# A state-space stage on one core: the scan's decay factors move into one ring of six buffers, made four units ahead

## What is computed

```python
hs, gate = split(einsum('blh,eh->bel', x, Win))            # 512 channels each
hs   = silu(conv4(hs) + bconv)
dt_in, Bm, Cm = split(einsum('bdl,pd->blp', hs, Wx))       # 128, 16, 16
dt   = softplus(einsum('blr,dr->bld', dt_in, Wdt) + bdt)
dA   = exp(A * dt)                                         # A = -exp(A_log), per channel and state
dBu  = dt * Bm * hs
h_t  = dA_t * h_(t-1) + dBu_t                              # per channel, state and step
y_t  = sum over the 16 states of h_t * C_t
y    = (y + hs * D) * silu(gate);  out = y @ Wout.T;  x = x + out
```

## Time and profile before

| | us |
|---|---|
| median of 3 runs | 4711.3 |
| lowest and highest run | 4702.89, 4714.27 |
| the profiled execution, its own time | 4701.33 |
| its span in the trace | 4699.5 |
| mean granted clock of TensorE, share of full | 0.939 |

### The profile page before, as it was taken

One profiled execution on the slowest core, in us unless ns is written; L12 is line 12 of the kernel. 1 busy time (PEld: TensorE's weight loads), 2 busy tenths in 40 slices (PEclk: granted clock), 3 DMA queues, 4 the chain that ended last, 5 costly groups with the idle time before them and its releaser, 6 DMA issues. The chain is left out here.

```text
span 4699.5 us, 147070 instructions
## 1 busy us (share of the span) xinstructions
PE 4031.9 (86%) x63660; PEld 2779.2 (59%) x63668; DVE 3046.8 (65%) x5625; ACT 2381.8 (51%) x4795; POOL 1496.9 (32%) x1590
## 2 busy tenths in 40 slices
PE   7627886678887887899799999999999998689999
PEld 6415654345565765344477777767776776455555
DVE  7897744757776887764577777777777776521111
ACT  3446533667776555322566666666666665221111
POOL 1001200168896221000344444444434443112222
PEclk9868987889998999999899999999999999789999
DMA  1000000123342000100110000001001000041111
GB/s 35 19 27 11 2 13 21 51 86 127 125 130 97 2 2 15 40 1 0 47 26 22 25 22 25 22 21 26 22 22 28 22 13 4 7 133 54 54 50 43
DMA packets 72986, 175.37 MB, mean 37 GB/s; under 512 B 14578, under 2 KB 27892, under 8 KB 69748
## 3 DMA queue, kind: packets, MB, share of 16 engines
q1 hardware_dynamic: 72340, 165.96, 11.5%
HBM read 163.04 MB, written 2.88 MB: 35 GB/s over the span
## 5 line engine op out<-in xcount | busy, mean ns | idle before, releaser
L3160 DVE TENSOR_TENSOR moe_hh<-moe_si,moe_pu 128x512 f32<-128x512 f32 x104 | 71.5, 688 | 450.5 <-PE moe_pu L3049 444.2
L1785 POOL TENSOR_TENSOR ssm_ub<-ssm_dtu,ssm_bcn 128x512 f32<-128x512 f32 x224 | 285.5, 1295 | 44.0 <-DMA ssm_bcn<-ssm_bct 29.7
L3093 ACT ACTIVATE moe_si<-moe_pg 128x512 f32<-128x512 f32 x104 | 62.1, 597 | 466.9 <-PE moe_pg L3049 466.9
L2601 POOL TENSOR_TENSOR dn_gm<-dn_cb,dn_cs 128x256 f32<-128x256 f32 x128 | 76.8, 621 | 666.7 <-DMA dn_cb<-dn_cum 436.0
L2617 POOL TENSOR_TENSOR dn_eb<-dn_ee,dn_cc 128x512 f32<-128x512 f32 x64 | 66.7, 1042 | 649.7 <-DVE dn_cc L2727 649.7
L3112 POOL TENSOR_TENSOR moe_hw<-moe_hh,moe_cb 128x512 f32<-128x512 f32 x100 | 126.6, 1266 | 444.7 <-DVE moe_hh L3160 392.8
L2368 PE MATMUL dn_po<-dn_wo,dn_cT 128*128 128x256 f32 x1024 | 244.4, 393 | 2.5 <-ACT dn_cT L2535 2.2
L1867 DVE TENSOR_TENSOR_SCAN ssm_hu<-ssm_da,ssm_ub 128x512 f32<-128x512 f32 x148 | 178.0, 1214 | 93.7 <-ACT ssm_da L1656 82.1
L2283 PEld LDWEIGHTS dn_pm<-dn_XB,dn_mb 32*32 32x32 f32 x16384 | 166.9, 105 | 112.1 <-issue 108.9
L2283 PE MATMUL dn_pm<-dn_zz,dn_XB 32*32 32x32 f32 x16384 | 208.6, 194 | 25.7 <-issue 25.7
L1722 ACT ACTIVATE ssm_ht<-ssm_ph,ssm_ct 128x128 f32<-128x128 f32 x640 | 182.6, 377 | 90.1 <-PE ssm_ph L1617 89.1
(11 more groups left out here) (511 smaller groups left out, 10914.0 us busy)
## 6 DMA issues: line engine op xcount, KB each, us to landing
ssm_bcn<-ssm_bct SPq DMA_DIRECT2D x128, 512.0 KB, 3.9
dn_cb<-dn_cum SPq DMA_DIRECT2D x32, 512.0 KB, 5.1
dn_w<-in_dn_w SPq DMA_DIRECT2D x32, 388.0 KB, 3.3
moe_cb<-moe_rows SPq DMA_DIRECT2D x64, 192.0 KB, 2.9
moe_w<-in_moe_w SPq DMA_DIRECT2D x26, 384.0 KB, 7.8
moe_cb<-moe_rows SPq DMA_DIRECT2D x64, 128.0 KB, 3.0
dn_wo<-in_dn_w SPq DMA_DIRECT2D x16, 256.0 KB, 5.6
moe_cb<-moe_rows SPq DMA_DIRECT2D x64, 64.0 KB, 2.6
```

The costliest lines, as they stand in the source:

```text
L1785: pool.tensor_tensor(ub[u % NUB][:, :], dtu[q % 2][:, c, :], bcn[i % NB][:, 0, :], ALU.mult).then_inc(ub_ready, 1)
L2601: last = pool.tensor_tensor(gm[i % 2][:, h::2, :], cb[i // NCH % 2][:, h, q, :, :], own, ALU.subtract)
```

## The change

All six factor buffers form one ring over all units: unit u takes slot u % 6, of which slots 0 and 1 are the two in PSUM and slots 2 to 5 the four in SBUF. ACT makes factor u+4 where it made factor u before (`LEAD` is 4), after waiting for scan u-2, the last that read that slot. The extra factors ahead of job `S` are gone, as four are always ahead.

```diff
-    NB, NUB, NHU, NHT, NDX = 4, 4, 2, 2, 4
+    NB, NUB, NHU, NHT, NDX, LEAD = 4, 4, 2, 2, 4, 4
...
-        silu_at = AT["S", 0]
-        apart = lambda u: 0 <= u % (IC * N) - silu_at < NDX
-        factor = lambda u: dx[:, u % (IC * N) - silu_at, :] if apart(u) else da[:, u % 2, :]
+        factor = lambda u: da[:, u % (NDX + 2), :] if u % (NDX + 2) < 2 else dx[:, u % (NDX + 2) - 2, :]
...
-                        if q:
-                            for n in range(NDX):
-                                decay((q - 1) * IC * N + silu_at + n)
...
+                def factors(u):
+                    k, n, cc = split(u)
+                    q, c = k // 2, k % 2 * 2 + cc
+                    if n == 0:
+                        act.wait_ge(dt_ready, q * IC + c + 1)
+                    if u >= NDX + 2:
+                        act.wait_ge(scan_done, u - NDX - 1)
+                    decay(u)
+
                 def unit(u):
-                    ahead_of(u)
+                    if u == 0:
+                        act.wait_ge(a_exp, 2)
+                        for v in range(LEAD):
+                            factors(v)
+                    if u + LEAD < NU:
+                        factors(u + LEAD)
                     scaled(u - 2)
...
-                def ahead_of(u):
-                    k, n, cc = split(u)
-                    q, c = k // 2, k % 2 * 2 + cc
-                    if u == 0:
-                        act.wait_ge(a_exp, 2)
-                    if n == 0:
-                        act.wait_ge(dt_ready, q * IC + c + 1)
-                    if apart(u):
-                        return
-                    if u >= 2:
-                        act.wait_ge(scan_done, u - 1 - (NDX if apart(u - 2) else 0))
-                    decay(u)
```

## The result

| | before | after |
|---|---|---|
| median of 4 runs, us | 4707.1 | 4802.61 |
| lowest and highest | 4701.05, 4714.27 | 4796.15, 4812.92 |
| span of the profiled execution | 4699.5 | 4794.4 |
| ratio, 95% interval | | 1.0204 (1.018 to 1.0229) |

All of it lies in the state-space stage: from the first scan's start to the last one's end it was 924.0 to 1484.5, 560.5 us, and is 926.4 to 1581.5, 655.0 us, +94.5. The 2.4 us by which it begins late are older than the first scan: the table change ahead of it (903.00 before) already stands at 905.44.

A forecast was written before the change was run, and what follows sets the result against it. The prediction took VectorE scans with two SBUF inputs and GpSimd products, running in turn, to bound the changed state-space stage. 122 - 10 + 12 = +124 us on 4701.3 gave 4825; with 10 for the runs' median, 4835, range 4800 to 4885.

The forecast's parts named there:

- The bound: State-space stage: DVE's scans with two SBUF inputs and POOL's products exclude each other; 170 such scans against 16 before.
- The price of a turn: State-space stage: each scan from SBUF adds 1.13 us to the turn-taking, beside 1.24 us for each POOL product.
- The check of 4.70 against 4.74 us: Earlier timeline from 994.66 us: two products and two scans took 4.70 us; run one after the other they make 4.74.
- the +122: Last four of the stage's five stretches: turn-taking without pause comes to 615.8 us against 494.0 before.
- The pauses: State-space stage: turn-taking pauses at jobs `S` while ACT is away, 3 us for each of four, +12 us.
- The first stretch: First 66.5 us of the stage: not bound by turn-taking, taken as 56 us between 48.3 and 66.5, -10 us.
- Nothing for ACT's slower writes, the order and the DMAs: ACT's factors into SBUF take 4.8 us more with 156 us free; instruction order and DMAs stay; no cost.
- A: Rival, state-space stage: DVE and POOL get by each other, POOL bounds; -68 us, about 4643; chance 0.04.
- B: Rival, scans from SBUF: each of 154 costs only 0.3 to 0.5 us; -20 to +50, say 4725; chance 0.06.
- C: Rival, state-space stage: ACT still hangs behind TensorE, DVE waits there, turns added; +202, 4913, half +160; chance 0.08.
- The signs named: Profile after: stage about 685 us, 170 scans around 2.2, 86 at 1.2, POOL over 85% busy, factor waits below 30.
- the step on waits: DVE in the stage: factors ready four units ahead, so most of its 117.7 us of waiting for them goes.

The follow-up runs named there:

- the placement alone: Kernel before, with factors in the ring of six but each made where it was made before, no lead: 4822.7 us against 4690.65, stage 672.5 us.
- the constant from SBUF: Kernel before, with all 256 scans reading a constant from SBUF in place of the factor, no lead: 4864.06 us, stage 731.2 us.

## Why the prediction was right, and where it was off

- **The bound.** That the profile's largest removable wait, 117.7 us of DVE for ACT, was not what mattered, and that DVE and POOL in turn would be the new bound: shown, by the placement alone (+112 without any lead) and by the constant from SBUF (+171).
- **The price of a turn**, taken as 1.13 us. This term was too large. The price in close alternation is 0.91, as the next product starts some 0.2 us before the scan's recorded end. The row was there: in the earlier trace rows the delayed product took 2.09, only 0.82 more than alone, and successive scans started 2.21 and 2.15 apart, not 2.37. The check of 4.70 against 4.74 us counted the last scan's tail and could not tell. With 0.91 the forecast's own sums are 163.9, 159.6, 159.6 and 97.9 for the last four stretches; measured: 170.7, 160.5, 160.5 and 99.9. That takes 35 us from the +122, and is most of what the forecast was off.
- **The pauses**, +12: the same four stretches exceed their sums by 10.6 us in all, so the size was near. The place was not: 3 us were put at each of four, and 6.8 lie in the second stretch and 0.9, 0.9 and 2.0 in the others.
- **The first stretch**, -10: 67.6 became 63.4, -4.2. ACT's waits for TensorE stayed, 34.2 us before and 30.1 after; that they set the length is argued and not tested.
- Together: 124 - 35 - 1.4 + 5.8 is 93.4, and 1.2 more come from the last four stretches before, which are 492.8 us when cut at unit 20's scan and not 494.0: the 94.5 measured, within rounding. Some luck is in it that the range held: 4802.6 lies 2.6 us above its lower end, and had the first stretch gained the 10 us counted on, with a turn priced a quarter too high, the time would have been below it. Of the 32 us below the forecast, 4 are the kernel before, whose median was taken as 4711.3 and is 4707.1.
- **Nothing for ACT's slower writes, the order and the DMAs**: ACT's busy time rose by 8 us with 243 us to spare, and nothing outside the stage moved.
- **The rivals.** A (DVE and POOL get by each other) and B (only the median's surcharge) fall by the 2.2 us medians. C was right in one half: DVE does wait for the transposes in place of some of the factors. (Half of POOL's idle time on top of 664 us gives +153, not the +160 written there; nothing rests on it.) Without the turns the lead is worth 17 us of the 68 that A's sum allowed.
- **The signs named**: 170 scans at 2.2 us, 86 at 1.2, POOL over 85% busy (579 of 655) came as said; the stage is 655 us and not 685. The waits for `ub` that were to replace those for factors came, some 35 us more. The 29.8 us of waiting for the transposes were named as the sign that the step on waits is wrong, and to that extent it is: the step left this wait out.

## What to carry to other kernels

Before a ring of buffers is extended from PSUM into SBUF, ask for each reader whether that gives VectorE a second SBUF input, and whether GpSimd works on SBUF products at that time: here one such scan costs the stage 0.72 us, and 154 of them six times what the deeper ring gave back. Where a few instructions of the wanted kind already stand in the trace, take their price from the distance of successive starts in close alternation, and look at both engines' rows, since the wait shows on whichever came second. A long wait on one engine's rows is not yet the gain; here 117.7 us were worth 17, since other waits moved in.

## What was not expected of the hardware

A scan from SBUF and a product in turn take 2.14 to 2.15 us where 1.13 and 1.24 us are their distances alone, so the exclusion does not last for the whole recorded duration of both, as the rule taken up in the prediction would have it. And a fill by GpSimd runs beside a scan with two SBUF inputs at full speed: medians of 1.20 to 1.22 us and none of 80 above 1.23, against 2.2 beside products.
